# Inner tiles of a double feed-forward ordered anew, with the third chunk's first head tiles ahead of the second projection

## The chip, the cores and the metric

One core of a Trainium2 chip runs the whole program. The metric is the device time of one execution in microseconds; lower is better. The engines are TensorE (PE, with its weight loads as PEld), VectorE (DVE), ScalarE (ACT), GpSimd (POOL) and SyncE (SP, which issues the DMAs). Each has its own instruction queue, worked off in order, and they meet only through semaphores.

## The reference

```python
def attention(x, W_qkv, W_out):            # x: 4 x 1024 x 512, 16 heads of 32
    q, k, v = split(x @ W_qkv.T, 3)
    q, k = elu(q) + 1, elu(k) + 1
    out = q * cumsum(k * v) / (q * cumsum(k) + 1e-9)   # along the sequence
    return out @ W_out.T * 32 ** -0.5

def ffn(x, w_gate_up, w_proj):             # hidden size 2048
    gate, up = split(x @ ternary_quant(w_gate_up).T, 2)
    h = rms_norm(silu(gate) * up)
    return h @ ternary_quant(w_proj).T

x = x + layernorm(attention(layernorm(x), W_qkv, W_out))
x = x + layernorm(ffn(layernorm(x), w_gate_up, w_proj))
```

`ternary_quant` takes groups of 64 weights: the scale is the mean of their absolute values, each weight is divided by it, rounded and clipped to -1, 0 or 1, and multiplied by it again.

## The kernel before

**Tiling.** The 4096 rows are four chunks of 512 columns, turned so that features lie on the 128 partitions. Chunks 0 and 1 are the two halves of one sequence, 2 and 3 of the next. A chunk's attention has 12 head tiles (`group(s, g)`, q, k and v for each of four j), 12 matmuls each, since every fp32 operand is split into a high and a low part (`..._hi` on ACT, `..._lo` on DVE). For each j, ACT makes Relu and Exp (`features`), DVE makes q and k (`front_features`), k times v (`front_products`), the running sums (`front_sums`), then the reciprocal and the output (`back_reciprocal`, `back_output`, `back_lo`). POOL makes numerator and denominator between them (`numden`). `project_att` multiplies by W_out; `stats_att`, `add_ln2`, `finish_x1`, `stats_x1` and `norm_x1` are the layernorms around it. `tile(s, j)` is the back of tile j with the front of j + 1 between its parts.

**Feed-forward.** 16 hidden tiles m a chunk. For each, PE makes a gate and an up `unit` (8 matmuls each), ACT takes the gate (`hidden_gate`), DVE multiplies by up (`hidden_value`), ACT and DVE write the high and low half (`hidden_hi`, `hidden_lo`), ACT squares (`hidden_square`), POOL adds the square up (`add_square`), and PE projects. `square_sums` and `read_square_sums` bring the sums of squares to the closing layernorm (`stats("f", ...)`, `rstd("f", ...)`, `add_final`, whose results are counted by `fin_x`).

**The double feed-forward.** Chunk 0 (f = 0) and chunk 1 (f = 1) go through it together, chunk 1 being `BEHIND` = 4 tiles late, so the inner tiles are m = 4 to 15 and n = m - 4. The 24 batches of raw weights are quantised in the same loops, in a ring of six places: ACT `cast(b)`, DVE `scale(b)` (group sums, scale, reciprocal, and for every second gate and up batch the `row_scales`), POOL `divide(b)` in `PARTS` pieces, DVE `ternary(b)` (clip and round), POOL `scale_back(b)` in `PARTS` pieces, DVE `diff(b)`. PE turns each batch in two halves (`transpose_half`) through the single bank `ps[3]`, and ACT copies each out (`put_half`). `turn` makes a diagonal matrix for it. An inner tile with even m turns two batches, one with odd m turns one. Units take banks 0 to 2 in turn, so a unit waits until the one three before it has been read. Chunk 0 projects in banks 4 to 7 in the loop. Chunk 1's hidden tiles are all kept (`hid_b`, the first eight of them where `tq`, `tk`, `tr` and `ts` lie), and it is projected in `attention_of_third`, where chunk 2's head tiles lie between its later tiles.

The order on every engine is written out by hand in its `start()`, and in `feed_forward_of_both` and `attention_of_third` for PE. Chunks 2 and 3 then go through `run_steps`, which the diff leaves as it is, but for the waits inside `features` and `out_hi`.

## Time and profile before

| | |
|---|---|
| median of 3 runs | 1240.16 us (1239.69 to 1240.44) |
| the profiled execution | 1242.1 us, of which the span from the first to the last instruction is 1239.8 us |
| mean granted TensorE clock | 0.963 of full speed |
| PE busy | 1110.7 us, 90% |
| PEld busy | 663.7 us, 54% |
| DVE busy | 793.0 us, 64% |
| POOL busy | 551.2 us, 44% |
| ACT busy | 442.6 us, 36% |

The profile is of one execution. A busy share is an average over stages that differ, so the windows of the stages say more than the table. In a row of the timeline the first two numbers are the start and the duration in us; the square bracket at the end is how long the engine was idle before it, and what ended that.

### The profile page before, as it was taken

How to read it: one execution, taken by the hardware profiler on the slowest of the kernel's cores; microseconds unless marked ns; L12 is line 12 of the kernel's file. 1: busy time of each engine (PE TensorE's matmuls, PEld its weight loads, DVE VectorE, ACT ScalarE, POOL GpSimd, SP SyncE). 2: the span in 40 equal slices, each digit the busy share in tenths (PEclk: the TensorE clock that was granted, in tenths of full speed). 3: DMA queues.
4: the chain of work that ended last, by engine and by line, in shares of the span. 5: the costliest groups of instructions: out<-in, count | busy, mean ns of one | idle time of the engine just before them, and what ended most of it. 6: DMA issues, size and time to landing. Idle time of an engine off the chain costs nothing. (4 is left out here: it accounts for less than half of the span.)

```text
span 1239.8 us, 14664 instructions
## 1 busy us (share of the span) xinstructions
PE 1110.7 (90%) x5315; PEld 663.7 (54%) x5376; DVE 793.0 (64%) x1248; ACT 442.6 (36%) x752; POOL 551.2 (44%) x612
## 2 busy tenths in 40 slices
PE   6995468887899959899999999999999999899997
PEld 6774334443445747444864477445854486454443
DVE  5999777778633676872687348843886278625423
ACT  4332055544541211443234422442234313333332
POOL 1546667778931254424343424441543344315322
PEclk9997689899999979999999999999999999899999
DMA  7020132111003002100210011000210020000000
GB/s 263 1 68 9 60 119 85 52 52 43 1 1 103 1 0 68 35 1 1 68 35 1 1 35 68 1 1 1 68 35 1 1 69 1 34 1 1 34 1 34
DMA packets 29079, 44.98 MB, mean 36 GB/s; under 512 B 1360, under 2 KB 9552, under 8 KB 29008
## 3 DMA queue, kind: packets, MB, share of 16 engines
q1 hardware_dynamic: 29008, 44.05, 11.0%
q8 instruction: 43, 0.70, 0.2%
q14 instruction: 28, 0.23, 0.1%
HBM read 34.60 MB, written 9.44 MB: 36 GB/s over the span
## 5 line engine op out<-in xcount | busy, mean ns | idle before, releaser
L516 PE MATMUL bank<-x3t,wgu_t 128*128 128x512 f16 x1536 | 353.1, 383 | 11.6 <-ACT ht L922 7.9
L1137 POOL TENSOR_TENSOR acc<-acc,ht 128x512 f32<-128x512 f32 x105 | 134.7, 1282 | 275.4 <-ACT ht L956 275.2
L516 PEld LDWEIGHTS bank<-x3t,wgu_t 128*128 128x128 bf16 x1536 | 149.2, 99 | 195.3 <-ACT ht L922 12.8
L552 PE MATMUL bank<-wproj_t,hid 128*128 128x512 bf16 x840 | 202.6, 381 | 6.4 <-ACT x3t_b L907 3.5
L1381 DVE TENSOR_TENSOR ht<-ht,bank 128x512 f32<-128x512 f32 x112 | 76.2, 680 | 176.2 <-PE bank L516 132.5
L497 PE MATMUL bank<-xnt,wqkv_hi 128*128 128x512 f32 x672 | 170.5, 396 | 4.9 <-DVE xnt L1394 3.3
L1085 POOL TENSOR_TENSOR tk<-tq,ts 128x512 f32<-128x512 f32 x32 | 65.2, 2037 | 183.4 <-DVE ts L1314 183.4
L552 PEld LDWEIGHTS bank<-wproj_t,hid 128*128 128x128 f16 x896 | 87.5, 98 | 107.1 <-issue 4.7
L497 PEld LDWEIGHTS bank<-xnt,wqkv_hi 128*128 128x128 f32 x672 | 126.4, 190 | 32.3 <-issue 4.3
L946 ACT ACTIVATE hid<-ht 128x512 f16<-128x512 f32 x112 | 70.5, 630 | 181.7 <-DVE ht L1381 181.7
L1387 DVE TENSOR_TENSOR hid<-ht,hid 128x512 f16<-128x512 f32 x112 | 91.5, 817 | 61.2 <-ACT hid L946 60.6
L1328 DVE RECIPROCAL tk<-tk 128x512 f32<-128x512 f32 x32 | 107.1, 3346 | 19.2 <-POOL tk L1088 19.2
L956 ACT ACTIVATE ht<-ht,grow 128x512 f32<-128x512 f32 x105 | 75.7, 721 | 91.6 <-DVE hid L1387 91.6
L497 PE MATMUL bank<-xnt,wqkv_lo 128*128 128x512 f32 x336 | 89.9, 389 | 0.0
L922 ACT ACTIVATE ht<-bank 128x512 f32<-128x512 f32 x112 | 65.5, 585 | 34.9 <-PE bank L516 34.8
L1054 POOL TENSOR_TENSOR yq<-wb,grs 128x256 bf16<-128x256 bf16 x96 | 69.3, 751 | 18.6 <-DVE grs L1218 18.6
L888 ACT ACTIVATE tr<-bank 128x512 f32<-128x512 f32 x32 | 19.2, 599 | 151.9 <-PE bank L497 120.2
L497 PEld LDWEIGHTS bank<-xnt,wqkv_lo 128*128 128x128 f32 x336 | 63.1, 188 | 13.3
L1061 POOL TENSOR_TENSOR yq<-yq,gsc 128x256 bf16<-128x256 bf16 x96 | 56.9, 623 | 25.9 <-DVE yq L1246 25.9
L516 PE MATMUL bank<-x3t_b,wgu_t 128*128 128x512 f16 x256 | 66.0, 405 | 0.0
L516 PE MATMUL bank<-x3t_last,wgu_t 128*128 128x512 f16 x256 | 57.5, 379 | 0.0
L604 PE MATMUL bank<-wout_hi,outt 128*128 128x512 f32 x192 | 53.3, 410 | 4.4 <-DVE outt L1342 4.4
(148 smaller groups left out, 1511.9 us busy)
## 6 DMA issues: line engine op xcount, KB each, us to landing
raw_q<-in_L_ffn_w_gate_up_dram SPq DMA_DIRECT2D x32, 256.0 KB, 2.8
xn<-in_L_attn_x_dram SPq DMA_DIRECT2D x7, 1024.0 KB, 5.3
out_dram<-xn SPq DMA_DIRECT2D x7, 1024.0 KB, 8.8
x<-in_L_attn_x_dram SPq DMA_DIRECT2D x6, 1024.0 KB, 6.5
raw_q<-in_L_ffn_w_proj_dram SPq DMA_DIRECT2D x16, 256.0 KB, 3.0
raw_a<-in_L_attn_W_qkv_dram SPq DMA_DIRECT2D x4, 768.0 KB, 8.6
xn<-in_L_attn_x_dram SPq DMA_DIRECT2D x4, 256.0 KB, 3.3
raw_out<-in_L_attn_W_out_dram SPq DMA_DIRECT2D x1, 1024.0 KB, 13.1
```

The source lines that it names most:

```text
L497: last = pe.matmul(bank[:], w[:, k, rows], xnt_of(s)[:, part_x, k], start=(n == 0), stop=(n == 3 * KD - 1))
L516: last = pe.matmul(bank[:], wgu_t[:, k, first_row:first_row + P], x[:, part, k], start=(n == 0), stop=(n == 2 * KD - 1))
L552: last = pe.matmul(bank[:], hid_of(f, part, k)[:, t * P:(t + 1) * P], wproj_t[:, k], start=(k == 0 and part == 0), stop=(k == MT - 1 and p ...
L922: act.activation(ht_of(f)[:, m % 2], pair_bank(f, m, 0, single)[:], ACT.Silu, scale=1.0 / SCALE3).then_inc(q["silu_done"], 1)
L946: act.activation(hid_of(f, 0, m), ht_of(f)[:, m % 2], ACT.Copy).then_inc(q["h_hi"], 1)
L956: act.activation(acc_of(f)[:] if m == 0 else h, h, ACT.Square, scale=grow[:, m:m + 1]).then_inc(q["sq_done"], 1)
L1054: pool.tensor_tensor(part(yq, i), part(wb, i), spread(grs[:, b % RING], i), ALU.mult).then_inc(q_y, 1)
L1085: pool.tensor_tensor(tk[:, d], tq[:, d], ts[:, d], ALU.mult).then_inc(den_mul, 1)
L1137: pool.tensor_tensor(acc[:], acc[:], ht_of(f)[:, m % 2], ALU.add).then_inc(q["acc_done"], 1)
L1328: dve.reciprocal(tk[:, d], tk[:, d]).then_inc(rec_done, 1)
L1381: dve.tensor_tensor(h, h, pair_bank(f, m, 1, single)[:], ALU.mult).then_inc(q["h_done"], 1)
L1387: dve.tensor_tensor(hid_of(f, 1, m), ht_of(f)[:, m % 2], hid_of(f, 0, m), ALU.subtract).then_inc(q["h_lo"], 1)
```

## The change

- **Inner tiles.** ACT squares chunk 1's tile n - 1 after the next tile's first `put_half` instead of squaring tile n at the end of its own. DVE's `scale` is cut into `scale_sums` and `scale_rest`. Where one batch is turned, `hidden_lo(1, n)` goes between the two; where two are turned, the first `scale` goes ahead of `hidden_value(1, n)` and `diff(b + 2)` ahead of `hidden_lo(1, n)`.
- **Row scales.** Four instructions instead of five. **`PARTS`** is 2 instead of 4: `divide` and `scale_back` are two instructions of 128x512 each.
- **Start.** The last of chunk 1's attention on POOL and DVE goes ahead of the first quantising work, and `turn(0)`, `turn(1)` go behind `out_hi(1, 3)`.
- **End of the inner tiles.** Projections 12 to 15 of chunk 0 go two by two into the first two of the last four tiles, `square_sums(0)` into the second, and `stats("f", 0)` into the third.
- **Third chunk.** Head tiles 0 to 2 of chunk 2 go ahead of the second chunk's projection, and projections 8 to 15 lie behind head tiles 3 to 10. For that, chunk 2's four feature buffers lie in `x3t` and `x3t_b` (`set_c`) and its attention output where `tq` to `ts` lie (`outt_c`). So `features(2, 0)` waits for all units, `out_hi(2, 0)` for eight projections of chunk 1, and `features(3, 0)` for chunk 2's whole output projection.

```diff
-        outt_c = [sb("outt_c_hi", [P, KD, N], F32R, at_x3t), sb("outt_c_lo", [P, KD, N], F32R, at_x3t_b)]
+        outt_c = sb("outt_c", [P, 2, KD, N], F32R, at_sets)
+        set_c = [sb(f"set_c{i}", [P, 2, N], F32, (at_x3t, at_x3t_b)[i // 2] + 8 * N * (i % 2)) for i in range(4)]
...
-        PARTS = 4
+        PARTS = 2
...  PE, last four tiles
                 for m in range(MT, MT + BEHIND):
                     k = m - MT
-                    project(0, m - BEHIND)
                     unit(1, m - BEHIND, 0)
+                    if k < 2:
+                        project(0, MT - BEHIND + 2 * k), project(0, MT - BEHIND + 2 * k + 1)
...
+                    if k == 2:
+                        pe.wait_ge(ss_read, 1)
                     transpose_x(2, (k,), lambda k: ps[3])
                     unit(1, m - BEHIND, 1)
+                    if k == 1:
+                        pe.wait_ge(xt_hi, at(KD, 2, k))
+                        pe.wait_ge(xt_lo, at(KD, 2, k))
+                        square_sums(0)
...  PE, attention_of_third
-                square_sums(0)
-                half = range(MT // 2)
-                for k in half:
+                for g in range(3):
+                    pe.wait_ge(fin_x, at(NT, 0, g))
+                    group(2, g, start=True)
+                square_sums(1)
+                pe.wait_ge(FF_SECOND["silu_done"], MT)
+                pe.wait_ge(FF_SECOND["h_done"], MT)
+                for k in range(KD):
                     wait_hid(1, k)
                     for t in range(NT - 1):
-                        if k == 0 and t == 0:
-                            pe.wait_ge(FF_SECOND["silu_done"], MT)
-                            pe.wait_ge(FF_SECOND["h_done"], MT)
                         project_tile(1, k, t)
-                pe.wait_ge(ss_read, 1)
-                square_sums(1, NT)
                 pe.wait_ge(ss_read, 2)
-                for k in half:
+                for k in range(KD):
                     project_tile(1, k, NT - 1).then_inc(FF_SECOND["pr_done"], 1)
-                for g in range(NG):
-                    if g < 4:
+                for k in range(KD, MT // 2):
+                    project_second(k)
+                for g in range(3, NG):
+                    if g == 3:
                         pe.wait_ge(fin_x, at(NT, 0, g))
                     else:
                         wait_group_read(pe, 2, g - 4)
                     group(2, g, start=True)
-                    k = MT // 2 + g
-                    if k < MT:
-                        wait_hid(1, k)
-                        for t in range(NT):
-                            last = project_tile(1, k, t)
-                        last.then_inc(FF_SECOND["pr_done"], 1)
+                    if MT // 2 + g - 3 < MT:
+                        project_second(MT // 2 + g - 3)
...  ACT, features
-                    if part == 0 and s == 2 and j < 2:
-                        act.wait_ge(FF_SECOND["pr_done"], MT // 2)
+                    if part == 0 and s == 2 and j == 0:
+                        act.wait_ge(FF_MAIN["up_done"], MT)
+                        act.wait_ge(FF_SECOND["up_done"], MT)
+                    if part == 0 and s == 3 and j == 0:
+                        act.wait_ge(out_done, 3 * NT)
...  ACT, out_hi
                 if j == 0 and s == 2:
-                    act.wait_ge(FF_MAIN["up_done"], MT)
-                    act.wait_ge(FF_SECOND["up_done"], MT)
+                    act.wait_ge(FF_SECOND["pr_done"], MT // 2)
...  ACT, start
-                cast(5), out_hi(1, 2), x3_hi(0), turn(0), turn(1), out_hi(1, 3)
+                cast(5), out_hi(1, 2), x3_hi(0), out_hi(1, 3), turn(0), turn(1)
...
-                    hidden_gate(1, m), put_half(first, 0), hidden_hi(1, m)
+                    hidden_gate(1, m), put_half(first, 0)
+                    if n > 0:
+                        hidden_square(2, n - 1)
+                    hidden_hi(1, m)
...
-                    hidden_square(2, n)
...
-                    hidden_gate(2, n), split_x(2, (m - MT,), lambda k: ps[3]), hidden_hi(2, n), hidden_square(2, n)
+                    hidden_gate(2, n), hidden_square(2, n - 1), split_x(2, (m - MT,), lambda k: ps[3]), hidden_hi(2, n)
+                hidden_square(2, MT - 1)
...  POOL, start
-                numden(1, 0), numden(1, 1), finish_x1(0), numden(1, 2), norm_x1(1)
-                divide(0), divide(1), numden(1, 3), scale_back(0), divide(2), scale_back(1), divide(3)
-                scale_back(2), divide(4), scale_back(3), rstd("2", 1), divide(5), finish_x1_rows(1, x1_b)
+                numden(1, 0), numden(1, 1), finish_x1(0), numden(1, 2), norm_x1(1), numden(1, 3)
+                divide(0), divide(1), scale_back(0), divide(2), scale_back(1), divide(3)
+                scale_back(2), divide(4), rstd("2", 1), scale_back(3), divide(5), finish_x1_rows(1, x1_b)
...
                 for m in range(MT - BEHIND, MT):
+                    if m == MT - 1:
+                        rstd("f", 0)
                     add_square(1, m)
...  DVE, row_scales
-                dve.tensor_scalar(power, bound, LEADING_BIT, None, ALU.mult).then_inc(q_bound, 1)
-                dve.tensor_tensor(rest, power, bound, ALU.subtract).then_inc(q_bound, 1)
-                dve.tensor_tensor(power, power, rest, ALU.subtract).then_inc(q_grow, 1)
+                dve.scalar_tensor_tensor(rest, bound, LEADING_BIT, bound, ALU.mult, ALU.subtract).then_inc(q_bound, 1)
+                dve.scalar_tensor_tensor(power, bound, LEADING_BIT, rest, ALU.mult, ALU.subtract).then_inc(q_grow, 1)
...  DVE, start
-                stats_x1(0), scale(0), scale(1)
-                tile(1, 2), x3_lo(0), ternary(0), scale(2)
-                back_reciprocal(1, 3), ternary(1), back_output(1, 3), scale(3), back_lo(1, 3)
-                diff(0), ternary(2), diff(1), scale(4), ternary(3)
+                stats_x1(0)
+                tile(1, 2)
+                back_reciprocal(1, 3), back_output(1, 3), x3_lo(0), back_lo(1, 3)
+                scale(0), scale(1), ternary(0), scale(2), ternary(1), diff(0), scale(3), ternary(2), diff(1)
                 stats_att(1, 4)
-                diff(2), scale(5)
+                scale(4), ternary(3), diff(2)
                 add_ln2(1, x1_b, lambda t: ps[4 + t][:])
+                scale(5)
...  DVE, inner tiles
+                    hidden_value(0, m), diff(b + 1), hidden_lo(0, m), ternary(b + 2)
+                    if twice:
+                        scale(b + 4), hidden_value(1, n), diff(b + 2), hidden_lo(1, n), ternary(b + 3), scale(b + 5)
+                    else:
+                        hidden_value(1, n), scale_sums(b + 4), hidden_lo(1, n), scale_rest(b + 4)
...  DVE, last four tiles
                     hidden_value(1, n), split_x(2, (m - MT,), lambda k: ps[3]), hidden_lo(1, n)
+                    if m == MT + 1:
                         read_square_sums(0)
+                    if m == MT + 2:
+                        stats("f", 0, lambda t: ps[4 + t][:], before_first)
                 add_final(0)
-                read_square_sums(1, NT)
-                front(2, 0, False, True)
+                front_features(2, 0), read_square_sums(1), front_products(2, 0, True), front_sums(2, 0, False)
```

## Rows read from the trace of the kernel before

**Rows 1.** Windows by stage: stretch, length, busy us (instructions) by engine, clock, DMA
```profile
106.76:195.01 88.25, 44.15 (x241) 28.48 (x242) 72.34 (x134) 30.95 (x59) 61.81 (x91) 0.75 0.22 70
195.01:351.60 156.59, 132.10 (x763) 65.80 (x775) 111.88 (x189) 78.73 (x141) 120.99 (x156) 0.93 0.14 42
...
372.50:448.40 75.90, 62.19 (x285) 40.80 (x289) 39.60 (x61) 12.62 (x21) 20.63 (x22) 0.95 0.13 42
...
477.10:1239.80 762.70, 734.49 (x3395) 421.25 (x3435) 454.14 (x703) 267.66 (x437) 290.91 (x282) 0.99 0.07 21
```

**Rows 2.** Waits from 106 to 196 us: total, times, longest
```profile
PE bank L604 <- issue: 22.6, 1, 22.6
```

**Rows 3.** Timeline of VectorE around the start
```profile
109.73 1.22 DVE L1213 TENSOR_REDUCE grs<-wb 128x16 f32<-128x1024 bf16 x1
...
139.15 0.98 DVE L1342 TENSOR_TENSOR outt_b<-tr,outt_b 128x512 fp32r<-128x512 f32 x1
...
163.81 0.69 DVE L1381 TENSOR_TENSOR ht<-ht,bank 128x512 f32<-128x512 f32 x1 [4.38 <-PE bank L516]
```

**Rows 4.** Waits in the inner tiles, 195 to 351 us
```profile
PE bank L486 <- ACT wgu_t L849: 22.8, 9, 4.8
ACT ht_b L956 <- DVE hid_b L1387: 22.7, 10, 4.4
```

**Rows 5.** Timeline of one stall, all engines
```profile
253.73 0.72 ACT L956 ACTIVATE ht_b<-ht_b,grow 128x512 f32<-128x512 f32 x1 [4.45 <-DVE hid_b L1387]
...
256.52 0.23 PE L486 MATMUL bank<-diag,wb 128*128 128x128 bf16 x1 [4.56 <-ACT wgu_t L849]
...
257.08 3.19 PE L516 MATMUL bank<-x3t_b,wgu_t 128*128 128x512 f16 x7
```

**Rows 6.** Window of one pair of inner tiles, m = 8 and 9
```profile
246.40:274.00 27.60, 22.10 (x127) 10.87 (x129) 19.50 (x34) 14.33 (x26) 21.32 (x29) 0.94 0.19 58
```

**Rows 7.** Timeline of GpSimd in a stretch without a gap
```profile
265.22 3.46 POOL L1054 TENSOR_TENSOR yq<-wb,grs 128x256 bf16<-128x256 bf16 x4 [3.93 <-DVE grs L1218]
...
276.92 2.32 POOL L1061 TENSOR_TENSOR yq<-yq,gsc 128x256 bf16<-128x256 bf16 x4
...
283.16 1.26 POOL L1137 TENSOR_TENSOR acc_b<-acc_b,ht_b 128x512 f32<-128x512 f32 x1
```

**Rows 8.** VectorE's operations alone and beside GpSimd's; last, their mean, 200 to 312
```profile
203.14 0.69 DVE L1252 TENSOR_TENSOR yq<-yq,wb 128x1024 bf16<-128x1024 bf16 x1
...
265.60 1.09 DVE L1252 TENSOR_TENSOR yq<-yq,wb 128x1024 bf16<-128x1024 bf16 x1
...
334.83 1.27 POOL L1137 TENSOR_TENSOR acc<-acc,ht 128x512 f32<-128x512 f32 x1
...
335.13 1.52 DVE L1252 TENSOR_TENSOR yq<-yq,wb 128x1024 bf16<-128x1024 bf16 x1
...
336.57 1.75 DVE L1387 TENSOR_TENSOR hid<-ht,hid 128x512 f16<-128x512 f32 x1
...
L1252 DVE TENSOR_TENSOR yq<-yq,wb 128x1024 bf16<-128x1024 bf16 x12 | 11.5, 955 | 1.3 <-POOL yq L1061 1.3
```

**Rows 9.** Timeline of TensorE: first and last of 13 projections' starts, m = 4 on
```profile
195.01 3.10 PE L552 MATMUL bank<-wproj_t,hid 128*128 128x512 bf16 x7 [3.51 <-ACT x3t_b L907]
...
350.11 1.67 PE L552 MATMUL bank<-wproj_t,hid 128*128 128x512 bf16 x7
```

**Rows 10.** Timeline around the third chunk's head tiles, TensorE and VectorE
```profile
374.02 1.02 PE L585 MATMUL bank<-columns,acc 128*128 128x1 f32 x8 [1.50 <-issue]
...
428.79 0.69 DVE L1305 TENSOR_TENSOR tr<-tk,bank 128x512 f32<-128x512 f32 x1 [2.68 <-PE bank L497]
...
448.37 3.41 PE L466 MATMUL bank<-ident_f,xn 128*128 128x128 f32 x16 [11.46 <-DVE tr L1305]
```

**Rows 11.** Timeline after the third chunk's attention, ScalarE, GpSimd and VectorE
```profile
465.17 0.58 ACT L888 ACTIVATE tr<-bank 128x512 f32<-128x512 f32 x1
...
480.11 0.20 POOL L1069 TENSOR_TENSOR vec<-vec 128x4 f32<-128x4 f32 x1
480.15 2.73 DVE L1357 SCALAR_TENSOR_TENSOR x<-bank,vec,x 128x512 f32<-128x512 f32 x4 [0.38 <-POOL vec L1067]
```

More of the change, by code:

```diff
@@ L127, in outt_of @@
         def outt_of(c, part):
-            return {1: outt_b[:, part], 2: outt_c[part][:]}.get(c, outt[:, part])
+            return {1: outt_b, 2: outt_c}.get(c, outt)[:, part]
         def hid_of(f, part, m):
@@ L577, in project, with project_second, square_sums @@
                 last.then_inc(q["pr_done"], 1)
-            def square_sums(f, first_column=0):
+            def project_second(k):
+                wait_hid(1, k)
+                for t in range(NT):
+                    last = project_tile(1, k, t)
+                last.then_inc(FF_SECOND["pr_done"], 1)
+            def square_sums(f):
                 q, c = ffn(f)
@@ L583, in square_sums @@
                 for t in range(NT):
-                    column = first_column + t
-                    last = pe.matmul(ps[3][:, column:column + 1], acc_of(f)[:, t * P:(t + 1) * P], ones[:], start=True, stop=True)
+                    last = pe.matmul(ps[3][:, t:t + 1], acc_of(f)[:, t * P:(t + 1) * P], ones[:], start=True, stop=True)
                 last.then_inc(ss_done, 1)
@@ L1141, in close @@
                 f = s - 1
-                rstd("f", f)
+                if s > 1:
+                    rstd("f", f)
                 x1_of = x1_last if do.last else x1
@@ L1465, in tile @@
                 back_lo(s, j)
-            def scale_from(b):
-                if b < NBATCH:
-                    scale(b)
             def start():
```

61 lines of the change are left out of this document (34 added, 27 removed).

## Prediction

> **What bounds the kernel now.** I read the windows by stage first, then the waits of each stage, then the timelines of the engines around the longest waits. The windows [rows 1] show three places where TensorE (PE) is not full: 44.2 of 88.3 us in the stretch that ends the second chunk's attention and starts the feed-forward, 132.1 of 156.6 us in the inner tiles m = 4 to 15, and 62.2 of 75.9 us around the second projection. After 477.1 us PE is 96% busy, and the diff touches nothing there but one wait. So the change can only earn in the first 477 us.
>
> In the first place one wait of 22.6 us ends at the output projection of chunk 1 [rows 2]. VectorE (DVE) has no gap there: it works off quantisation (from 109.73 us, for 5.6 us) ahead of the reciprocal of (1,2), and writes the last low half at 139.15 [rows 3].
>
> In the second, PE's wait is 22.8 us in sum for ScalarE's (ACT) copy of a turned weight half, while ACT waits 22.7 us in its square of the second chunk's hidden tile for DVE's low half [rows 4]. One case is laid out in [rows 5]: DVE's low half comes behind the whole scale work; ACT's square then starts at 253.73 after 4.45 us, the cast and the next gate follow, and PE turns the next half at 256.52 after 4.56 us idle. The 7 multiplications behind it take 3.19 us, at the lower clock. This costs about 4.5 + 1.5 us in each full pair of inner tiles. A pair runs 27.6 us, in which PE is busy 22.1, DVE 19.5 and GpSimd (POOL) 21.3 [rows 6]: no engine is full, the order is the bound.
>
> **The change, step by step.**
>
> 1. *Start.* norm_x1(1), numden(1,3) and the reciprocal, output and low half of (1,3) pass ahead of scale(0), scale(1), ternary and so on. Taken off the path to 139.15: quantisation from 109.73 to 115.28 (5.6 us), and about 6.5 us of the same between 128.0 and 139.1. Walking the queues with the rows' durations, the reciprocal of (1,2) starts at 109.8, POOL's denominator of (1,3) is ready at 120.7, the reciprocal ends at 124.0, output, four x3 low halves (2.5) and the low half follow by 128.1: the projection starts 12 us earlier. But the quantisation is now behind it. scale(0) to diff(1) fill DVE to 142.2, then come the statistics; POOL's rstd("2",1) now stands behind divide(4), whose scale comes after those statistics, so add_ln2 starts near 150.3 and scale(5) ends at 154.6. The first hidden product, 163.81 before [rows 3], starts then: 9.2 us earlier. What follows is bound by DVE and POOL in the same order. I take 8.3 (0.9 off for the longer POOL pieces, below); bounds 6 and 12.
>
> 2. *Inner tiles, ACT and DVE.* hidden_square(2,n-1) moves behind the next put_half(first,0), and hidden_lo(1,n) goes ahead of the row scales. In the case of [rows 5], ACT would go from the high half (about 249) straight to the cast, the gate at about 250.4 and the copy at 250.9; PE ends its unit at 251.96 (256.52 less 4.56). The 4.5 us stall and the cold clock behind it go. PE would then need 19.9 us a pair (8 units of 1.73, 16 projection products of 0.216, 6 turned halves of 0.44). Next late are POOL and DVE. POOL ran without a gap from 265.22 to 284.42 (19.2 us) for five of a pair's six quantising calls and all four additions [rows 7]; with the sixth (2.3) 21.5.
>
> 3. *PARTS 4 to 2.* 24 POOL pieces a pair become 12 of double length. Two pieces follow each other in 2 x 0.58 = 1.16 us, the 128x512 addition takes 1.26 [rows 7], and the smallest tensor_tensor 0.20 [rows 11]. No row has 128x512 in bf16: between 12 x 0.10 lost and 12 x 0.20 won; I take 0.6 won, as a piece's 0.58 is mostly elements. POOL: 20.9 a pair. [...]
>  The other side is DVE. A diff alone takes 0.69; beside 0.58 us pieces 1.09; beside a 1.26 us addition 1.52, and the low half after it 1.75 instead of 0.69 [rows 8]. So an op that meets a double piece loses some 0.54 us more. A pair has about 18 such (3 diffs, 6 ternary ops, 4 low halves, 5 small ones): nothing to 9.7 us. By the mean of the diffs in the inner tiles (0.955, [rows 8]) two thirds meet a piece now; but DVE's reduces and products, over which POOL's pieces pass unmet, take 7 us of a pair, so I take a little under half: 4.5.
>
> 4. *Row scales, 4 instructions instead of 5:* one of about 0.54 a pair, 0.5 saved. DVE: 19.5 - 0.5 + 4.5 = 23.5 us a pair. That is the new bound, over POOL's 20.9 and PE's 19.9.
>
>  The inner tiles take 155.1 us now, from the first projection product at 195.01 to the tail's at 350.11 [rows 9]; the starts of every second tile between them give pairs of 23.3, 28.1, 27.5, 28.0, 26.4 and 21.9. After: 22.5, 23.5, 23.5, 25.5 (it holds stats_x(2), 3 us of DVE that lay in a gap), 23.5 and 20.8 = 139.3. Gain 15.8; by POOL's floor 27.6.
>
> 5. *End of the inner tiles.* Projections 12 to 15 move, at the same cost. square_sums(0) comes inside: 1.0 us (374.02 row, [rows 10]) and a wait for DVE's product and split of about 1.5, so the last unit ends 2.5 later, 375.0. stats("f",0), 3.1 us, now lies between hidden values 14 and 15; product 15 comes 1.3 late, then split, low half and add_final: fin_x(0,0) at 379.1. The head tiles wait on it, 4.1 us against 1.5 now, and start cold, 1.8 more, as in [rows 5].
>
> 6. *Third chunk.* From the last unit to the last head tile: 12 x 2.72 + 16 x 1.73 + 1.0 = 61.3, plus 5.9, ends 442.2 (now 436.9). PE's turning of x waits for k·v of the fourth group, now at 448.37 after 11.46 idle [rows 10]. That follows from head tile 8 by 19.3 us of DVE and POOL (product 428.79, stats_x(3), norm_x(3), numden, reciprocal). Tile 8 will end 13.4 before the last, as projections now lie between the last tiles: 428.8, so 448.1. Net nothing (0.3): the earlier heads fill PE, not this chain. Bounds: 5 won if the heads don't wait, 4 lost if the sums come later.
>  out_hi(2,0)'s wait for eight projections (404) is over long before its tile (416). The new wait of features(3,0) for the projection moves them from 465.17 to 477.1; queued behind are DVE's features, then add_ln2, which waits for POOL until 480.15 anyway [rows 11]: 0 to 0.2 lost, hidden. SP's loads follow casts and stores as before.
>
> Sum: 8.3 + 15.8 + 0 = 24.1. The profiled execution took 1242.1 us (span 1239.8): 1218.0. The median of the three runs is 1.9 below it, 1240.16: 1216.
>
> **Rivals.**
>
> - *The port is fuller than I take it.* If POOL and DVE's readers of SBUF pairs fully exclude each other, a pair needs 24 x 0.58 + 4 x 1.26 = 18.9 plus 3 x 0.69 + 3 x 0.84 + 4 x 0.69 = 7.4, so 26.3. The loop then gains 5, the sum is 13: 1227. For it: the stretched ops of [rows 8]. Against: from 265.22 POOL took only 2.6 over its undisturbed 16.6 while DVE did some 14 such ops. Chance 0.2.
>  The Trainium skill (SBUF — State Buffer, "SBUF: two separate sides") states this as a rule, an exclusive lock in which the loser fully blocks; the trace agrees only in part, by that 2.6.
> - *POOL's floor holds*, the double pieces cost DVE nothing more: loop gain 27.6, start 8.3: 1204. For it: PE and ACT have the room. Against: [rows 8]. Chance 0.17.
> - *The heads don't wait* for fin_x, and the chain from tile 8 starts 5 earlier: 1211. Chance 0.08.
> - *Slower.* Every one of the 18 DVE ops waits for a whole double piece: 19.0 + 9.7 = 28.7 busy, and with 3 of today's 8 us of gaps left 31.7 in each of four full pairs, 24 and 23 in the others: 174 against 155. Less the 8.3: 1240 + 11 = 1251. It decides from a mean pair of 27.2 (25.85 + 8.3/6). Against: POOL would then idle a third of the time, and ops would meet fewer pieces. Chance 0.06.
> - *No change:* the stalls move to other waits and the start's gain is given back by quantisation, 1240. Chance 0.04.
>
> **How the numbers follow.** My forecast has 0.45 (1211 to 1223 by itself). The low end 1203 is just under the floor rival; the high end 1230 takes in the port rival with a start of only 6; outside are the slow ones and half of what lies beyond either end. What a measurement can tell from no change is 0.2%, 2.5 us. Faster 0.9, same 0.04, slower 0.06.
>
> **What would show it.** The projection of chunk 1 at 128 instead of 140.2, the first hidden product near 155. PE's wait for ACT's copies under 5 us in the inner tiles, pairs of 23.5 with DVE over 90% busy, diffs at 1.2 us or more in the mean. First head tile 4 us after the last unit; x turned after about 6 us idle, 24 earlier than now. Wrong if pairs stay above 26, if scale(5) still runs after 158, or if the turning of x comes more than 3 us off the shift of the last unit.

## The result, and the profile after

The changed kernel takes 1228.82 us in the median of four runs (1226.97 to 1232.95), beside 1240.3 us for the kernel before on the same chip: a ratio of 0.9909, with a 95% interval of 0.988 to 0.9937. It is faster, by 11.5 us where 24.1 were forecast: inside the predicted 1203 to 1230, near its slow end. The profiled execution, from which the rows come, took 1232.95 us (span 1231.2), 4.1 above the median and 9.15 below the profiled execution of before.

The windows of the changed kernel by stage, and by pair of inner tiles (columns as in [rows 1]; the first two answer to [rows 1], the pairs to [rows 6]):

```profile
106.76:192.46 85.70, 45.77 (x242) 28.81 (x242) 80.69 (x131) 31.87 (x59) 61.37 (x59) 0.76 0.22 72
192.46:339.15 146.69, 127.84 (x768) 64.00 (x769) 126.45 (x182) 77.11 (x141) 105.35 (x93) 0.95 0.15 45
192.46:214.88 22.42, 22.15 (x129) 10.77 (x130) 19.68 (x31) 10.85 (x22) 14.65 (x14) 0.91 0.28 90
214.88:237.98 23.10, 20.43 (x129) 10.29 (x128) 22.69 (x33) 14.03 (x27) 17.63 (x16) 1.00 0.23 69
237.98:262.20 24.22, 20.61 (x129) 10.22 (x128) 23.81 (x33) 14.10 (x28) 19.35 (x17) 1.00 0.21 66
262.20:289.15 26.95, 21.57 (x129) 10.98 (x128) 25.92 (x43) 14.47 (x28) 19.91 (x18) 0.94 0.17 50
289.15:319.13 29.98, 23.06 (x129) 11.29 (x128) 25.34 (x34) 12.95 (x23) 24.20 (x23) 0.89 0.00 1
319.13:339.15 20.02, 20.02 (x129) 10.45 (x128) 9.02 (x13) 10.71 (x19) 9.61 (x9) 1.00 0.01 2
339.15:365.96 26.81, 25.31 (x121) 12.64 (x119) 9.14 (x15) 9.51 (x16) 5.75 (x5) 0.94 0.00 0
365.96:439.55 73.59, 63.32 (x281) 40.95 (x281) 37.67 (x58) 12.70 (x21) 21.11 (x23) 0.95 0.14 44
```

The reader is to see two things. In the pairs from 214.88 and 237.98, DVE is busy for 22.69 of 23.10 and 23.81 of 24.22 us: 98%, with the clock at 1.00. It is the new bound, and a full pair went from 27.6 to 23 or 24 us. The pair from 289.15 is the odd one: 29.98 us, DVE idle for 4.6 us of them and PE for 6.9.

TensorE's timeline at the four points that answer to [rows 2], [rows 9] and [rows 10]: the projection of chunk 1, that of the fifth hidden tile, the first head tile, and the turning of the fourth chunk's x.

```profile
128.63 2.04 PE L616 MATMUL bank<-wout_hi,outt_b 128*128 128x512 f32 x4 [9.17 <-issue]
...
192.46 3.57 PE L558 MATMUL bank<-wproj_t,hid 128*128 128x512 bf16 x8 [5.30 <-DVE x3t_b L1412]
...
370.09 3.37 PE L503 MATMUL bank<-xnt,wqkv_hi 128*128 128x512 f32 x8 [4.07 <-DVE x L1450]
...
439.55 3.65 PE L472 MATMUL bank<-ident_f,xn 128*128 128x128 f32 x16 [6.20 <-DVE set_c L1345]
```

The first stands 11.6 us earlier than before, the second only 2.5, the last 8.8. The inner tiles, from 192.46 to the tail's first unit at 339.15, are 8.4 shorter than before. So two of the three amounts that the sum was made of are short: 8.3 forecast against 2.5, and 15.8 against 8.4.

VectorE at the start of the changed kernel, which answers to [rows 3]:

```profile
129.69 0.17 DVE L1252 TENSOR_SCALAR gsc<-grs 128x16 bf16<-128x16 f32 x1
...
131.33 0.97 DVE L1252 TENSOR_SCALAR gsc<-grs 128x16 bf16<-128x16 f32 x1
...
132.85 0.89 DVE L1268 SCALAR_TENSOR_TENSOR shrink<-row_bound 128x2 f32<-128x2 f32 x1
133.78 0.97 DVE L1270 SCALAR_TENSOR_TENSOR grow<-row_bound,shrink 128x2 f32<-128x2 f32 x1
...
139.63 1.53 DVE L1290 TENSOR_TENSOR yq<-yq,wb 128x1024 bf16<-128x1024 bf16 x1
...
155.61 2.73 DVE L1401 SCALAR_TENSOR_TENSOR x_b<-bank,vec,x_b 128x512 f32<-128x512 f32 x4 [0.99 <-POOL vec L1089]
...
159.91 0.67 DVE L1425 TENSOR_TENSOR ht<-ht,bank 128x512 f32<-128x512 f32 x1
```

An instruction over 16 columns, 0.17 us when it meets nothing (129.69), takes 0.97; the two-sided subtraction `diff` takes 1.53, where it is 0.69 alone [rows 8]. add_ln2 starts at 155.61, not 150.3, and the first hidden product at 159.91, not near 155.

The costly pair on three engines. GpSimd first: the norm of the third chunk's x (`norm_x(2)`) stands in its queue ahead of a `scale_back`, and the four calls follow each other without a gap until 309.7:

```profile
301.47 3.02 POOL L1099 TENSOR_SCALAR xn<-xn,vec 128x512 f32<-128x512 f32 x4 [0.21 <-POOL vec L1091]
304.46 2.04 POOL L1083 TENSOR_TENSOR yq<-yq,gsc 128x512 bf16<-128x512 bf16 x2
306.45 2.04 POOL L1076 TENSOR_TENSOR yq<-wb,grs 128x512 bf16<-128x512 bf16 x2
308.45 1.26 POOL L1160 TENSOR_TENSOR acc<-acc,ht 128x512 f32<-128x512 f32 x1
```

VectorE in the same stretch:

```profile
306.52 3.73 DVE L1290 TENSOR_TENSOR yq<-yq,wb 128x1024 bf16<-128x1024 bf16 x1 [3.42 <-POOL yq L1083]
```

And TensorE:

```profile
310.31 0.29 PE L492 MATMUL bank<-ident_b,wb 128*128 128x128 bf16 x1 [5.31 <-DVE yq L1290]
...
311.14 3.62 PE L522 MATMUL bank<-x3t,wgu_t 128*128 128x512 f16 x8
```

The `diff` waits 3.42 us for its `scale_back` and then lasts 3.73 us where 0.69 would do: it ends 0.5 us after GpSimd's run of calls ended (308.45 + 1.26 = 309.71). An instruction that lasts several times its usual length, until GpSimd's run is over, is called held below. PE stands for 5.31 us, and the unit behind takes 3.62 us instead of 1.89: the granted clock is 0.50 from 310.31 to 314.80, and was 1.00 from 303.11 to 305.00.

### The profile page after: what moved, and what is told of

Read it like the earlier page. It is cut to its first block and busy times, and to the rows that moved or that the text cites. A ratio compares the mean times of both kernels' runs of the same rounds, so it can differ in the third digit from the quotient of the medians.

```text
span 1231.2 us, 14622 instructions
## 1 busy us (share of the span) xinstructions
PE 1116.3 (91%) x5376; PEld 665.3 (54%) x5376; DVE 817.1 (66%) x1240; ACT 442.4 (36%) x752; POOL 535.6 (44%) x516
## 5 line engine op out<-in xcount | busy, mean ns | idle before, releaser
L558 PE MATMUL bank<-wproj_t,hid 128*128 128x512 bf16 x896 | 211.1, 381 | 5.3 <-DVE x3t_b L1412 5.3
L1431 DVE TENSOR_TENSOR hid<-ht,hid 128x512 f16<-128x512 f32 x112 | 98.8, 882 | 60.8 <-ACT hid L965 60.5
L1108 POOL TENSOR_TENSOR tk<-tq,ts 128x512 f32<-128x512 f32 x28 | 58.1, 2074 | 147.4 <-DVE ts L1355 147.4
L1370 DVE RECIPROCAL tk<-tk 128x512 f32<-128x512 f32 x28 | 93.7, 3346 | 10.8 <-POOL tk L1111 10.8
L1076 POOL TENSOR_TENSOR yq<-wb,grs 128x512 bf16<-128x512 bf16 x48 | 54.6, 1157 | 25.3 <-DVE grs L1254 25.3
L522 PE MATMUL bank<-x3t_b,wgu_t 128*128 128x512 f16 x256 | 62.9, 392 | 0.0
L1083 POOL TENSOR_TENSOR yq<-yq,gsc 128x512 bf16<-128x512 bf16 x48 | 49.7, 1056 | 27.4 <-DVE yq L1282 27.3
```

What stands on the lines that cost most here:

```text
L522: last = pe.matmul(bank[:], wgu_t[:, k, first_row:first_row + P], x[:, part, k], start=(n == 0), stop=(n == 2 * KD - 1))
L558: last = pe.matmul(bank[:], hid_of(f, part, k)[:, t * P:(t + 1) * P], wproj_t[:, k], start=(k == 0 and part == 0), stop=(k == MT - 1 and p ...
L1108: pool.tensor_tensor(tk[:, d], tq[:, d], ts[:, d], ALU.mult).then_inc(den_mul, 1)
L1370: dve.reciprocal(tk[:, d], tk[:, d]).then_inc(rec_done, 1)
L1431: dve.tensor_tensor(hid_of(f, 1, m), ht_of(f)[:, m % 2], hid_of(f, 0, m), ALU.subtract).then_inc(q["h_lo"], 1)
```

## The experiments

The kernel before had medians of 1241.02, 1241.13, 1240.84 and 1240.99 us beside the four groups in which they ran, so the groups agree to about half a microsecond. A single median is known less well: its interval is 1 to 2 us either way, and 3.5 us for the changed kernel. Differences of 2 or 3 us between two medians are therefore weak, and those from the changed kernel most of all.

"The projection" below is the first one of the inner tiles (195.01 before, 192.46 changed). It moves a little too: the changed kernel, e2, e3 and e7 have the same order of work up to there, and it came at 192.46, 190.70, 192.03 and 192.21; in the kernel before and e6, at 195.01 and 193.90. "In the trace" below means the one profiled execution.

**Four pieces in the changed kernel (e1).**

```diff
-        PARTS = 2
+        PARTS = 4
```

> The changed kernel with PARTS at 4 again. Piece theory (the double pieces on GpSimd make every VectorE operation that meets one wait some 0.5 us longer): the quantising work between 128 and 147 us shortens by 3 to 5 us, the first inner tile starts near 188 instead of 192.5, VectorE is less busy in each pair of inner tiles, and the whole takes 4 to 9 us less than the changed kernel, 1220 to 1225. Rival (fewer, longer pieces relieve GpSimd, which is what the inner tiles need): the whole takes 2 to 5 us more, 1231 to 1234, and GpSimd is over 21 us busy a pair. If both cancel: within 2 us.

Measured: 1224.0 us (1223.35 to 1225.64), ratio 0.9862 [0.9849, 0.9874], 4.8 less than the changed kernel. The projection came at 189.3 instead of 192.5, and the pairs at 21.8, 22.3, 23.1, 27.9, 29.0. By the projections (190.7 to 192.5 for this order with double pieces) 1.4 to 3.2 us of what they cost lay ahead of the inner tiles, and 0.8 and 1.1 us in the second and third pair; the fourth took 1.0 less with them. The odd pair keeps its stall with either size. VectorE's busy time in the second and third pair, here with four pieces:

```profile
211.13:233.41 22.28, 20.45 (x129) 10.29 (x128) 20.83 (x33) 14.00 (x26) 20.70 (x27) 1.00 0.23 71
233.41:256.52 23.11, 20.53 (x129) 10.20 (x128) 21.62 (x33) 13.93 (x26) 22.75 (x29) 1.00 0.22 69
```

So the double pieces add 1.9 and 2.2 us of busy time (22.69 and 23.81 with them), and take 3.1 and 3.4 us off GpSimd's (17.63 and 19.35). With four pieces GpSimd is as full as VectorE in the third pair, 22.75 of 23.11 us.

**The norm moved off the odd pair (e2).**

```diff
-                    if m == 11:
+                    if m == 14:
                         norm_x(2)
```

> The changed kernel with GpSimd's norm_x(2) behind tile m = 14 instead of m = 11. Queue theory (its 5 us stand ahead of a scale_back for which VectorE's diff and then TensorE wait): the pair m = 12, 13, now 30.0 us, falls to 23 to 25, and the whole to 1223 or so, 5 us less. Rival (VectorE's diff is shut out from the shared port by chance, wherever GpSimd's work lies without a gap): the stall of 5.3 us turns up elsewhere and the whole stays within 2 us of 1229.

Measured: 1223.38 us (1223.04 to 1225.5), ratio 0.9858 [0.9846, 0.9871], 5.4 less than the changed kernel. The pair of tiles 12 and 13 in its windows:

```profile
288.10:309.10 21.00, 20.26 (x129) 10.38 (x128) 20.59 (x30) 9.77 (x19) 16.13 (x15) 1.00 0.01 2
```

21.0 us instead of 30.0 (28.4 in both e3 and e7, and 26.7 in e4, which keep the order of that pair). The spans differ by 10.0 us, the medians by 5.4: the changed kernel's profiled execution is its longest, and the medians are the better measure. The stall is two things. In e4 the queue is the same, with the same wait of 3.42 us, but the `diff` is not held:

```profile
308.34 1.51 DVE L1290 TENSOR_TENSOR yq<-yq,wb 128x1024 bf16<-128x1024 bf16 x1 [3.42 <-POOL yq L1083]
```

So the queue is worth some 5.7 us of the pair (26.7 against 21.0), and the `diff` held for 3.73 us the other 1.7 to 3.2. This stall is the largest single thing that the prediction did not have.

**The third chunk and the tail as before (e3)**: PE's last four tiles, `attention_of_third`, the buffers, and the DVE and POOL order behind the inner tiles in their old form.

> The changed kernel with the end of the inner tiles and the third chunk as before (projections 12 to 15 one by one, sums of squares and statistics behind the last unit, head tiles behind half of the second projection, buffers as before). Forecast of the sum: nothing, so within 1.5 us of the changed kernel. From the traces: the tail takes 4.5 us more and the third chunk 2.3 less, so undoing both gains about 2: 1227. Rival (the early head tiles earn several us that show only in the total): 1232 or more.

Measured: 1229.5 us (1228.45 to 1231.01), ratio 0.9905 [0.9892, 0.9918], 0.7 from the changed kernel. Moving the head tiles ahead earned nothing that can be measured, as forecast in step 6.

**The start as before (e4)**: the first of chunk 1's head outputs and the quantising in the old order on DVE, POOL and ACT.

> The changed kernel with the start's order as before (quantising work ahead of the last of chunk 1's attention), all else changed. Forecast of the sum: 8.3 lost, 1237. From the traces: the start earned 2.5, so 1231. With double pieces both orders pay for them, so what is lost may lie between: 3 to 8. If the order at the start is worth nothing: 1229.

Measured: 1231.34 us (1230.75 to 1235.96), ratio 0.9925 [0.991, 0.994], 2.5 more than the changed kernel, with overlapping intervals; the projection at 193.9, 1.4 later. This run alone can't size the start to a microsecond (in its trace the odd pair was 3.2 shorter, as no `diff` was held in it), but with the projection only 1.4 later it speaks against 8.3; e13 settles it.

**The two pieces alone, in the kernel before (e5).**

```diff
-        PARTS = 4
+        PARTS = 2
```

> The kernel before with PARTS at 2 and nothing else. Piece theory: at the start the quantising ops of VectorE lie on the path (VectorE has no gap there) and in the inner tiles the low half of chunk 1 waits behind row scales whose three small ops each meet a double piece, some 0.4 us longer each: 3 to 9 us more than before, 1243 to 1250. Rival (GpSimd gains 12 times 0.13 us a pair and VectorE has 8 us of gaps a pair): within 2 us of before or 2 to 4 less.

Measured: 1256.74 us (1255.03 to 1257.17), ratio 1.0128 [1.0114, 1.0142]: 15.6 slower, beyond the 1243 to 1250 that was expected. Its waits in the inner tiles (total, times, longest) answer to [rows 4]:

```profile
PE bank L486 <- ACT wgu_t L849: 30.7, 9, 6.9
ACT ht_b L956 <- DVE hid_b L1387: 26.9, 10, 5.4
```

PE's wait grew by 7.9 us. In the old order DVE's scale work lies in the chain from the low half over ACT's square to the copy that PE waits for [rows 5]. That would put all that a double piece holds up there on the path, and in the new order only part of it; the size is measured, this reason is argued.

**The inner order alone (e6)**: DVE's and ACT's order of the inner tiles in the kernel before, with four pieces and five row-scale instructions.

> The kernel before with the inner tiles' order alone (ACT's square behind the next copy, scale cut in two, low half ahead of the row scales), PARTS 4, row scales of five instructions, start and third chunk as before. Forecast of the sum: 155.1 us of inner tiles become about 139, 1224. From the run with four pieces, where they took 144: 11 less than before, 1229. If the gain of the order needed the rest of the change: under 5 less, 1236 or more.

Measured: 1229.99 us (1229.43 to 1231.14), ratio 0.9916 [0.9903, 0.993]. This one part gives 11.1 us, as much as the whole change, and the inner tiles took 11.1 us less in the trace too (144.0 against 155.1).

**The fourth chunk's statistics behind the first head tile (e7).**

```diff
-                tile(2, 0), tile(2, 1), stats_x(3), tile(2, 2)
+                tile(2, 0), stats_x(3), tile(2, 1), tile(2, 2)
```

> The changed kernel with VectorE's stats_x(3) one tile earlier (behind tile(2,0) instead of tile(2,1)), GpSimd's order unchanged, so that norm_x(3) is done before the third tile's sums. Chain theory (TensorE's idle time before it turns the last chunk is the chain head tile 8, product, stats_x(3), norm_x(3), numden, reciprocal): the 6.2 us idle falls to 0 to 1 and the whole takes 4 to 6 us less, 1223 to 1225. Rival (VectorE is full there, the 3 us only move): within 1 us of 1229.

Measured: 1226.49 us (1225.24 to 1228.17), ratio 0.9888 [0.9874, 0.9901]; 2.3 less than the changed kernel by the medians, with overlapping intervals and above the 1223 to 1225 that was expected; 4.8 less by the profiled spans (1226.4 against 1231.2). Its TensorE timeline at the turning of x:

```profile
433.87 1.94 PE L472 MATMUL bank<-ident_f,xn 128*128 128x128 f32 x16 [0.98 <-DVE set_c L1345]
...
440.60 3.75 PE L503 MATMUL bank<-xnt,wqkv_hi 128*128 128x512 f32 x8 [4.80 <-DVE xnt L1438]
```

The idle time fell from 6.20 to 0.98 us; the wait behind it grew from 3.10 to 4.80, while the turning itself took 1.94 us at a granted clock of 1.00, against 3.65 at 0.50. The chain named in step 6 was the right one, and the statistics in it was the link that could go.

**The combined kernel (e8)**: e1, e2 and e7 together, and on POOL the rstd of chunk 1's norm one call earlier.

```diff
-                scale_back(2), divide(4), rstd("2", 1), scale_back(3), divide(5), finish_x1_rows(1, x1_b)
+                scale_back(2), rstd("2", 1), divide(4), scale_back(3), divide(5), finish_x1_rows(1, x1_b)
```

> The changed kernel with PARTS 4, norm_x(2) behind m = 14, stats_x(3) one tile earlier, and rstd of chunk 1's second layernorm ahead of divide(4). If the four add: 4.8 + 5.4 + 5 + 2 = 17 us less, 1212. If the first two repair the same stall of the pair m = 12, 13: 1214 to 1217.

Measured: 1210.47 us (1208.25 to 1212.85), ratio 0.9758 [0.9743, 0.9773]. It beats both kernels: 30.7 us under the kernel before, 18.4 under the changed one. The single edits come to 12.5 by their medians (4.8, 5.4, 2.3), or 15 with e7 by its span. That the combined kernel wins more than their sum isn't established: each of the three is measured from the changed kernel's median, and if that kernel were 3 us slower than its median, which its interval allows, the sum would be the whole 21 us.

**The combined kernel with five row-scale instructions (e9)**

> The combined kernel with the row scales in their old form (one multiplication, three small instructions, one reciprocal instead of one, two scalar_tensor_tensor, one reciprocal). Theory A, that the merged form costs as much as it saves (0.97 and 0.89 us for the two against three of 0.53 in the trace): the time is within 1 us of the combined kernel's 1210.5, on either side. Theory B, the prediction's own term (0.54 us a pair less work on the full engine, six pairs and the start): 3 to 4 us slower, 1214.

Measured: 1213.67 us (1213.34 to 1214.66), ratio 0.9781 [0.9768, 0.9794]: 3.2 slower, the size that theory B gives. But 2.3 us of it stand already at the projection (189.7 against 187.4), and the six inner pairs took only 0.8 more (139.9 against 139.1), 0.14 a pair and not 0.5. On the way to the projection a `diff` is held here:

```profile
176.28 4.01 DVE L1292 TENSOR_TENSOR yq<-yq,wb 128x1024 bf16<-128x1024 bf16 x1 [1.15 <-POOL yq L1083]
```

and not in the combined kernel:

```profile
176.00 1.08 DVE L1290 TENSOR_TENSOR yq<-yq,wb 128x1024 bf16<-128x1024 bf16 x1 [1.49 <-POOL yq L1083]
```

So the trace doesn't bear out theory B's reason: this one meeting, 2.9 us longer, is as large as nearly the whole difference.

**The combined kernel with two pieces (e10)**

> The combined kernel with each scale_back in two pieces of 512 columns instead of four of 256. Theory A, that VectorE is full and each of its operations that meets a double piece is held back up to 1.04 us instead of 0.58: 5 to 12 us slower than the combined kernel, 1216 to 1222, with the mean of the two-sided subtraction and of the hidden value's low part up by 0.2 to 0.4 us. Theory B, the prediction's step 3 (0.6 us a pair won on GpSimd, 0.54 us a meeting lost): no more than 4 us slower, under 1215.

Measured: 1220.09 us (1216.95 to 1220.59), ratio 0.9831 [0.9817, 0.9844]: 9.6 slower, theory A in time; the mean of the low part rose by 0.33 us as it says, that of the `diff` only by 0.09 (1.03 to 1.12). The instruction that writes the scale, over 16 columns, by its groups between 200 and 312 us (busy, mean ns), here with two pieces:

```profile
L1252 DVE TENSOR_SCALAR gsc<-grs 128x16 bf16<-128x16 f32 x14 | 10.5, 749 | 0.3
```

and in the combined kernel with four:

```profile
L1252 DVE TENSOR_SCALAR gsc<-grs 128x16 bf16<-128x16 f32 x13 | 5.4, 419 | 0.3
```

It costs 0.33 us more each time, for an instruction that has 16 elements a partition to write.

**The combined kernel with the old third chunk (e11)**

> The combined kernel with the tail and the third chunk's head tiles in the old order (head tiles 0 to 2 in the walk behind the half projection, not ahead of it), statistics of the fourth chunk still behind the first tile. Theory A, that the early head tiles earn only once the chain behind head tile 8 is freed: 3 to 8 us slower than the combined kernel, 1213 to 1218, all of it between the tail's last unit and the turning of the fourth chunk's x. Theory B, that they are worth nothing here either, as in the changed kernel (1229.5 without them against 1228.8 with them): within 1.5 us of 1210.5.

Measured: 1207.73 us (1206.88 to 1209.22), ratio 0.9733 [0.972, 0.9746]: 2.7 faster than the combined kernel by the medians, with intervals that just touch; neither theory had it. Its turning of x:

```profile
416.03 3.65 PE L466 MATMUL bank<-ident_f,xn 128*128 128x128 f32 x16 [3.15 <-DVE tr L1320]
```

In the kernel before, in the same order of head tiles, that wait was 11.46 us [rows 10], and 11.48 in e3. What went was the statistics between, not the place of the head tiles. The new place costs the 4.07 us ahead of the first head tile; from about 314 us, where both kernels start tile 15's projection (314.6 and 314.1), to the turning of x it takes 103.7 us, the old place 101.9: 1.8 of the 2.7 stand in the traces. PE is busy for 96.7 and 96.6 of them.

**The tail's gaps filled (e12)**: in the combined kernel, `stats("f", 0)` and `add_final(0)` a hidden value earlier on DVE, and their rstd a call earlier on POOL.

```diff
                     n = m - BEHIND
+                    if m == MT + 2:
+                        stats("f", 0, lambda t: ps[4 + t][:], before_first)
+                    if m == MT + 3:
+                        add_final(0)
                     hidden_value(1, n), split_x(2, (m - MT,), lambda k: ps[3]), hidden_lo(1, n)
                     if m == MT + 1:
                         read_square_sums(0)
-                    if m == MT + 2:
-                        stats("f", 0, lambda t: ps[4 + t][:], before_first)
-                add_final(0)
...  POOL
-                    if m == MT - 1:
+                    if m == MT - 2:
                         rstd("f", 0)
```

> The combined kernel with the statistics of the first feed-forward's output placed at the start of the tail's last tile, ahead of the hidden value, and the first residual sum ahead of the last hidden value, so that the head tiles find their banks free. Theory A, that TensorE's 4.1 us wait ahead of the head tiles is for this statistics and sum on VectorE, which idles earlier in the tail: the wait falls to 2.5 us or less and the cold first unit (3.4 us) goes warm, 2 to 4 us faster than the combined kernel, 1206 to 1209. Theory B, that the two instructions now hold up the hidden values behind them by as much: the unit of the tail's last tile is 2 to 4 us later and the time stays within 1.5 us of 1210.5.

Measured: 1207.17 us (1205.73 to 1211.4), ratio 0.9733 [0.9715, 0.9751]; by the medians 3.3 less than the combined kernel, but the intervals overlap, and the profiled executions are equal (spans 1209.6 and 1209.3). TensorE's last unit and first head tile here:

```profile
350.12 1.89 PE L522 MATMUL bank<-x3t_b,wgu_t 128*128 128x512 f16 x8
354.26 2.49 PE L503 MATMUL bank<-xnt,wqkv_hi 128*128 128x512 f32 x8 [2.25 <-issue]
```

and in the combined kernel:

```profile
348.03 1.89 PE L522 MATMUL bank<-x3t_b,wgu_t 128*128 128x512 f16 x8
353.99 2.75 PE L503 MATMUL bank<-xnt,wqkv_hi 128*128 128x512 f32 x8 [4.07 <-DVE x L1450]
```

The wait fell by 1.8 and the unit ahead of it came 2.1 later: what theory B says, in the trace. Whether the timed 3.3 us are the edit's stays open.

**The start by itself (e13 to e15)**: in the kernel before, first the start's order alone; then the merged row scales as well; then the two pieces as well.

> The kernel before with the start's order alone (heads' outputs ahead of the quantising on VectorE, GpSimd's and ScalarE's order with it), four pieces and old row scales. Theory A, that the order gains near the forecast 8.3 us and the double pieces took it: the projection that stood at 195.01 starts at 187 to 189, and the time is 6 to 8 us under the kernel before if the inner tiles keep it. Theory B, that the quantising chain was costed too short whatever the pieces (its small instructions meet GpSimd's pieces where they had not before): 190.5 to 193, and 2 to 5 us.

> The same with the merged row scales. Theory A, that with four pieces they save what the prediction said (half a microsecond for each batch on VectorE): the projection 1.5 to 2.5 us earlier than in the run with the order alone, and 2 to 4 us less in all. Theory B, that the merged instructions cost what they save: within 0.5 us of it there, within 1 us in all.

> The same with two pieces as well. Theory A, that the double pieces took the start's gain: the projection at 191.5 to 193 as in the changed kernel (192.46), 3 to 5 us later than with four pieces; and in the inner tiles, which keep their old order, the loss is near that of the two pieces alone (15.6 us), so the time is above the kernel before, 1243 to 1252. Theory B, that it is the inner order's doing: the projection within 1.5 us of the run with four pieces.

Measured: 1238.27 us (1236.55 to 1239.43), ratio 0.9977 [0.9967, 0.9986]; 1231.08 (1230.86 to 1232.11), 0.9923 [0.9911, 0.9935]; 1253.42 (1251.58 to 1253.91), 1.0098 [1.0085, 1.0112]. The projection with the order alone:

```profile
192.14 3.42 PE L552 MATMUL bank<-wproj_t,hid 128*128 128x512 bf16 x8 [3.50 <-DVE x3t_b L1368]
```

with the row scales:

```profile
188.89 2.38 PE L552 MATMUL bank<-wproj_t,hid 128*128 128x512 bf16 x8 [1.46 <-ACT x3t_b L907]
```

and with the double pieces:

```profile
191.39 3.57 PE L552 MATMUL bank<-wproj_t,hid 128*128 128x512 bf16 x8 [5.30 <-DVE x3t_b L1366]
```

So 195.0 becomes 192.1 by the order, 188.9 by the row scales, and 191.4 by the pieces; the changed kernel, with the inner order as well, stands at 192.5. Theory B holds for the first: the order never had 8.3 us in it. Of the other two theory A has the sign, but both moved the time beyond its ranges. The pieces cost 22.3 us here (e15 against e14), more than the 15.6 of e5, and 1253.4 is above the 1243 to 1252 that was expected.

The row scales' 7.2 us in all, for 2 to 4 expected, are more than the eight pairs of batches times 0.54 explain (4.3). The rest can be seen in the traces. GpSimd's four pieces and VectorE's `diff` with the order alone:

```profile
178.64 2.32 POOL L1054 TENSOR_TENSOR yq<-wb,grs 128x256 bf16<-128x256 bf16 x4
...
178.71 4.02 DVE L1252 TENSOR_TENSOR yq<-yq,wb 128x1024 bf16<-128x1024 bf16 x1 [1.69 <-POOL yq L1061]
```

and the same two with the row scales:

```profile
177.41 3.40 POOL L1054 TENSOR_TENSOR yq<-wb,grs 128x256 bf16<-128x256 bf16 x4
...
177.49 1.08 DVE L1250 TENSOR_TENSOR yq<-yq,wb 128x1024 bf16<-128x1024 bf16 x1 [1.49 <-POOL yq L1061]
```

Both engines are at the same instructions, VectorE 0.07 or 0.08 us behind. In one kernel it is shut out over all four pieces and the addition behind them, in the other it gets in behind the first piece, and GpSimd's next ones take longer instead (3.40 us for the four). These 2.9 us are as much as nearly all of the 3.3 by which the projection comes earlier, and with the 4.3 they would make the 7.2; no run has the two apart. What decides who gets in isn't shown; so an edit that moves such a meeting can win or lose 3 us by it, which is luck and not the edit's work.

**The rstd behind the divide again (e16)**, in the combined kernel.

> The combined kernel with the reciprocal root of the feed-forward's norm on GpSimd behind the fifth divide, as in the changed kernel. Theory A, that it stood in front of the first hidden tile's scaled input and the 6 us beyond the single runs' sum come partly from there: 1.5 to 3 us slower, 1212 to 1213.5, the output of the first hidden tile on VectorE later by as much. Theory B, that it lies beside other work: within 1 us of 1210.5.

Measured: 1212.92 us (1211.11 to 1215.43), ratio 0.9776 [0.9759, 0.9793]. By the medians 2.4 slower, with overlapping intervals; the spans are equal (1209.3 both). The projection comes 1.6 later (189.0 against 187.4), and by the next one the lead is gone (200.0 against 199.7). Not settled; whether there is any excess of the combined kernel over its single edits to explain is open as well (e8).

## Why the prediction was short

**What held.** The projection of chunk 1 at 128.6 (128.1 forecast). The 4.5 us stalls of [rows 4, 5] are gone from most tiles: PE's longest wait for ACT's copy left in the inner tiles is 4.57 us, once, behind `stats_x(2)`; their sum is 13.0 us against 22.8, more than the 5 that were named. DVE is the new bound: 22.7 and 23.8 us busy in the two undisturbed full pairs, for 23.5 forecast. The first three pairs came at 22.4, 23.1 and 24.2 (22.5, 23.5, 23.5), the last at 20.0 (20.8). The first head tile waits 4.07 us (4.1), the turning of x 6.20 (about 6), and the stretch from the last unit to it is 73.6 us, with 73.1 from the prediction's times (448.1 less 375.0).

**Right by luck.** DVE's 23.5 us a pair were summed as 19.5 - 0.5 + 4.5, all of the 4.5 for meetings with double pieces. The double pieces are worth 1.9 and 2.2 (e1). The rest is there with four pieces too: DVE's busy time in the second and third pair goes from 19.3 and 19.4 us in the kernel before to 21.1 and 21.9 with the inner order alone (e6). The prediction carried the 19.5 over from a pair with gaps. That the two engines meet more often once the gaps are closed is the likely reason, and is argued here; the rise itself is measured.

**Step 1 failed, by 5.8 us.** The order's part was mis-sized: 8.3 forecast, 2.9 measured with four pieces (e13), and 2.5 with all of the change in. Two terms did it. The quantising chain was costed at 14.1 us, too little for instructions that now stand one behind another and meet POOL's at nearly every step: it took 17.2 us with single pieces (127.96 to 145.15, e13) and 18.6 with double ones (128.44 to 147.02). So scale(5) ran to 159.9, past the 158 that the prediction had named, and the first hidden product started at 158.3 in e13 and 159.9 here, not near 154.6. The wait for POOL's rstd behind the fifth divide, 2.1 us in e13 and 1.0 here, is no extra term: the 150.3 for add_ln2 has about 2 us of it.

The second term is that what follows the first hidden product was to keep the whole lead. In e13 5.5 us of lead at that product are 2.9 at the projection. POOL is the likely reason, though no run isolates it: it ends the scaled rows of x_b at 164.7 in e13 and at 161.9 in the kernel before, so it is later and not earlier, and DVE waits 0.59 us for it at 162.72. The 0.9 us taken off for longer pieces was too little as well: e15 against e14 gives 2.5 at the projection. A share of luck went the other way: the kernel before has a `diff` held for 4.02 us at 181.36, which the prediction did not see, and the changed kernel has none at the start (1.51 us at 179.46). A slip in step 1 cost nothing: the quantising taken off the path between 128.0 and 139.1 is 7.3 us by the timeline of the kernel before, not 6.5.

**Step 3 missed a queue, by 6.5 us.** The pair of tiles 12 and 13 was forecast at 23.5 and took 29.98. `norm_x(2)` had been in POOL's queue before too, but the prediction never asked what was queued behind it once DVE and PE had no slack left. e2 brings that pair to 21.0 us and takes 5.4 off the time. Some 5.7 us of the pair are the queue, the rest is the held `diff` behind it (e4). The pair before it took 1.5 more than forecast, behind `stats_x(2)` on DVE. These two are the whole of the inner tiles' miss (8.0, less 0.5 in the others, against 15.8 - 8.4 = 7.4). Both pairs are above the 26 that the prediction named as a sign of its being wrong.

**Step 3's terms.** POOL won more than 0.6 us a pair: two double pieces take 2.04 and four single ones 2.32 [rows 7], 0.28 for each of six calls, 1.7 a pair at 0.14 us for each instruction dropped; with fewer stretched pieces its busy time fell by 3.1 and 3.4 us (e1). It earned nothing, as POOL is not the bound. As an edit, the two pieces cost 4.8 us here (e1), 9.6 in the combined kernel (e10), and 15.6 and 22.3 in the old inner order (e5, e15 against e14). The rival of the fuller port gave 1227, near the measured time, but not by its mechanism: it wanted 26.3 us in every full pair, and the undisturbed ones took 23.1 and 24.2. For the rival of POOL's floor, the gain of 27.6 has no working: six pairs of 20.9 us would give 29.7.

**Step 4.** The 0.5 us a pair is not borne out in time: 0.14 a pair in the combined kernel (e9). In the old inner order the row scales won 3.6 us over the six pairs (154.7 to 151.1, e13 and e14), 0.6 a pair, but there they lie ahead of the low half. Beside the double pieces the two merged instructions take 0.89 and 0.97 us, more together than the three old ones beside single pieces (0.52, 0.53 and 0.54 in e13).

**Steps 5 and 6.** The tail ran from 339.15 to 365.96, 4.5 us longer than before where 2.5 were forecast: beside the 1.5 wait and the 1.0 of the sums, the unit behind them was slow (3.12 us for 1.89, at a granted clock of 0.58), which the prediction had priced for the head tiles and not here. From the last unit to the turning of x it gained 2.3 (75.9 to 73.6), with 2.8 forecast. In all some 2.1 lost, where the forecast had nothing: 2.55 + 8.4 - 2.1 = 8.8, by which the turning of x is earlier. The rest of the 9.15 between the profiled executions lies behind it.

## What to carry to other kernels

- When a cure makes an engine the bound, read the queues of the others again for what had been covered by the old stall: here 4.9 us of a norm on GpSimd, in the queue at the same place before, cost 5.4 us, where the whole inner order gave 11.1.
- Price instructions that will run back to back beside another engine by rows where they already meet it, not by their rows alone. Small ones suffer most in proportion, and where one engine is full, its partner's instructions should be short: the same edit of piece size cost 5, 10, 16 or 22 us by what stood around it.
- Filling a gap with work from elsewhere only moves the gap if the chain behind it keeps its length. One statistics out of the chain did more (5.2 us of idle time) than three head tiles moved ahead of it, which in the end cost about 2 (1.8 by the traces, 2.7 by the medians).
- Before crediting an edit with 3 us, look in both traces for a single long hold that one of them happens to miss: it stands in e13 and not in e14, in e9 and not in the combined kernel.

## What the hardware showed that was not expected

- A two-input DVE instruction can be held for the whole of a gap-free run on GpSimd: 3.73 us at 306.52, where GpSimd went from one `divide` into an addition. The kernel before has one too, at 181.36 us, 4.02 us long; so have e1, e3, e6, e7, e9 and e13, always the `diff`, and the other runs have none. Single meetings cost it only up to about 0.85 us (1.53 against 0.69), so a mean hides it. With VectorE starting 0.07 or 0.08 us behind GpSimd it went either way (e13 and e14).
- DVE instructions over 2 or 16 columns, 0.17 us alone, can take nearly as long as the GpSimd piece that they meet: up to 0.58 us with pieces of 0.58, up to 0.98 (1.19 in e5) with pieces of 1.02.
